# Widening in float32 on quarters of the array where no convolution runs beside it, and in four float16 products elsewhere

## The chip, the cores and the metric

The kernel runs on one core of a Trainium2 chip. The metric is the device time of one execution in microseconds (us); smaller is better. The core has five instruction streams that run on their own and wait for one another by semaphores: TensorE (PE, whose weight loads are listed as PEld), VectorE (DVE), ScalarE (ACT), GpSimd (POOL) and SyncE (SP, which only starts DMAs here).

## The reference

The input is 32 images of 64 channels and 112 x 112 pixels in float32. Two residual layers follow one another:

```
x = x + conv3x3(groupnorm(x), sign(weight) * alpha)
h = w_in (256 x 64) . groupnorm(x)                    # per pixel
h = irfft2(rfft2(8 x 8 patches of h) * fft_filt)      # per channel
h = depthwise 3x3 (h, w_dw)
x = x + w_out (64 x 128) . (gelu(h[:128]) * h[128:])  # per pixel
```

Group normalisation has 32 groups, so pairs of channels. The step that this document is about is `w_in`: 64 channels are widened to 256.

## The kernel before

Images are taken in 16 pairs (64 channels of either image make the 128 partitions) and each image in 14 strips of 8 rows. The kernel is a software pipeline over steps t = 0 to 13 for each pair: step t transposes and transforms strip t (`front`), widens, filters and evaluates strip t-1 (`mid`), interpolates strip t-2 (`up`) and projects strip t-3 (`done`). In steps 6 to 12 the binary convolution of the next pair runs as well, two strips in each; the last pair has no next one. So a strip whose widening falls in such a step is of kind "conv", each other of kind "plain": 105 strips are conv, and 119 are plain (7 of 14 in each of 15 pairs, and all 14 of the last pair). Statistics of the next pair (`bn_stats`) are taken by DVE in steps 0 to 4; the tiny matmuls that average the statistics over pairs of channels (`groups`) stand in steps 5 and 13.

Every engine's order is written out by hand in a function `image` for it, one branch for conv steps and one for plain ones. What one strip goes through in `mid`:

- `pixels` (ACT, line 464) copies the transposed strip to the tile xT; `forward_transform` (PE, line 930) turns it into the patch basis with float32 matmuls on four quarters of the array (64 rows and 64 columns each); `spectrum` (ACT, line 469) copies the result back to the same tile, then called xf.
- `spectrum_high` (ACT, line 478) rounds xf to float16, xf_hi; `spectrum_low` (POOL, line 351) makes the rest, xf_lo. w_in is held in the same way as win_hi and win_lo.
- `widened` (PE, line 941), in four groups of two, two, two and one of the strip's seven blocks of 16 columns, called W0, W1, W2 and W3 here. In a plain step their order is W3, W2, W1, W0. A block takes four products in float16 (hi.hi, lo.hi, hi.lo, lo.lo), each for both images on the upper and the lower half of the array's rows, which run side by side.
- `filtered` (DVE, line 690) multiplies each group with the filter into hf. W1 waits until the filtered W3 has left its PSUM banks, and W0 until the filtered W2 has.
- `evaluated` (PE, line 953), float32 on quarters of the array, in four groups for each image; `weighted` (DVE, line 697) multiplies each into one of three buffers of v32; `high_nodes` (ACT, line 487) and `low_nodes` (POOL, line 357) split it into v_hi and v_lo in float16.
- `interpolated` (PE, line 971) in the step after; then `carried0` and `gated` (DVE, 706, 713, 722), `gelu`, `keep0` and `keep1` (ACT, 507, 511, 516); `projected` (PE, 985), `lifted` (ACT, 494), `residual` (POOL, 364).

A group of v is written here as (image, group), so v(1,3) is the first of the second image. POOL's order in a plain step is residual, v_lo(0,3), residual, v_lo(0,2), (0,1), (0,0), (1,3), then xf_lo, then v_lo(1,0), (1,1), (1,2). The reuse of the three buffers of v32 ties DVE to POOL: `weighted` (1,3) waits until v_lo(0,2) is done, (1,0) until (0,1) is, and the next strip's (0,3) and (0,2) until v_lo(1,1) and (1,2) are:

```
V_BUF = {"plain": [{3: 0, 2: 1, 1: 2, 0: 0}, {3: 1, 0: 2, 1: 0, 2: 1}],
...
                nc.gpsimd.tensor_tensor(xf_lo[:], xf[:], xf_hi[:], ALU.subtract).then_inc(pool_xl, 1)
```

Of the kernel before, what the change touches and what calls it, by code (L numbers as in the profile page):

```python
# [8 lines left out]
ALU = mybir.AluOpType  # L9

P = 8
C = 64
C2 = 256
HC = 128
# [57 lines left out]
def shape_constants():  # L72

    basis, picks = patch_basis()
    pick = np.zeros((P * (P // 2 + 1), BPX))
    for patch in range(2):
        for f, (a, b) in enumerate(picks):
            pick[a, patch * P * P + f] += 0.5
            pick[b, patch * P * P + f] += 0.5
    samples_at, taps_at, back = toom_cook()  # L80
    nodes = np.zeros((P * P, 128))
    nodes[:, :POINTS] = basis.T @ np.kron(samples_at, samples_at).T

# [11 lines left out]
def build(nc, x, conv_w, alpha, w_in, w_dw, filt, w_out, forward, pick, pair, apart, identity, nodes, taps, ext, out):  # L95
    B, _, H, W = x.shape
    PAIRS = B // 2
    STRIPS = H // ROWS
# [8 lines left out]
    IMGS = 2  # L107
# [25 lines left out]
    with ctx:  # L133
        def sb(name, shape, dt=F32):
            return ctx.enter_context(nc.sbuf_tensor(name, shape, dt))
# [51 lines left out]
        filt_sb = v32[0:NF, 0, 1, 0, :]  # L187
        win_sb = v32[:, 2, 0, 0, :]
        c_taps = v32[0:9, 0, 0, 1, 0:128]
# [57 lines left out]
        pe_out = sem("pe_out")  # L247
        N_CONST = 15
        N_CONV = 4
# [33 lines left out]
        def _(sp):  # L283
# [10 lines left out]
            for dst, src in ((c_fwd[:], forward), (c_pick, pick), (c_pair[:], pair), (c_apart[:], apart), (c_id[:], identity),  # L294
                             (c_nodes[:], nodes), (c_taps, taps), (ext32, ext), (filt_sb, filt), (wdw_sb, w_dw),
                             (wout_sb[:], w_out), (win_sb[0:C], w_in), (win_sb[C:128], w_in)):
                sp.dma_start(dst, src).then_inc(dma_const, 16)
# [31 lines left out]
        def _(pool):  # L329
# [37 lines left out]
            def image(n, par, prev, front, more):  # L367
                for t in range(STRIPS if front else OUT):
                    mid = item(n, t, MID, prev, front)
                    done = item(n, t, OUT, prev, front)  # L370
                    if more and CONV_FROM <= t <= CONV_TO:
# [21 lines left out]
                    else:  # L393
# [10 lines left out]
                        if mid:  # L404
# [3 lines left out]
                            low_nodes(mid[0], mid[1], 1, 3)  # L408
                        if front:
                            spectrum_low(n, t)  # L410
# [20 lines left out]
        def _(act):  # L431
# [86 lines left out]
            def image(n, par, prev, front, more):  # L518
                for t in range(STRIPS if front else OUT):
# [3 lines left out]
                    if more and CONV_FROM <= t <= CONV_TO:  # L523
# [42 lines left out]
                    else:  # L566
# [20 lines left out]
                        if front:  # L587
                            spectrum(n, t, BANK_P)
                            spectrum_high(n, t)
                        if mid:  # L590
# [30 lines left out]
        def _(dve):  # L621
# [12 lines left out]
            def groups_x(n):  # L634
                dve.wait_ge(pe_grpx, n + 1)
                nc.vector.tensor_copy(groupx[:], Z[:, 0:3]).then_inc(dve_grpx, 1)
                dve.wait_ge(dve_grpx, n * 4 + 1)
                nc.vector.scalar_tensor_tensor(out=varx[:], in0=groupx[:, 2:3], scalar=groupx[:, 2:3],
                                               in1=groupx[:, 1:2], op0=ALU.mult, op1=ALU.add).then_inc(dve_grpx, 1)
                dve.wait_ge(dve_grpx, n * 4 + 2)  # L640
                nc.vector.tensor_scalar(vex[:], varx[:], 0.0, GN_EPS, ALU.max, ALU.add).then_inc(dve_grpx, 1)

            def shift_x(n):
                dve.wait_ge(pool_rstdx, n + 1)
                nc.vector.scalar_tensor_tensor(out=nbx[:], in0=groupx[:, 0:1], scalar=-1.0, in1=rstdx[:],
                                               op0=ALU.mult, op1=ALU.mult).then_inc(dve_grpx, 1)
# [5 lines left out]
            def groups_1(n):  # L652
                dve.wait_ge(pe_grp1, n + 1)
                nc.vector.tensor_copy(group1[:], Z[:, 0:3]).then_inc(dve_grp1, 1)
                dve.wait_ge(dve_grp1, n * 4 + 1)
                nc.vector.scalar_tensor_tensor(out=var1[:], in0=group1[:, 2:3], scalar=group1[:, 2:3],
                                               in1=group1[:, 1:2], op0=ALU.mult, op1=ALU.add).then_inc(dve_grp1, 1)
                dve.wait_ge(dve_grp1, n * 4 + 2)
                nc.vector.tensor_scalar(ve1[:], var1[:], 0.0, GN_EPS, ALU.max, ALU.add).then_inc(dve_grp1, 1)

            def shift_1(n):
                dve.wait_ge(pool_rstd1, n + 1)
                nc.vector.scalar_tensor_tensor(out=nb1[:], in0=group1[:, 0:1], scalar=-1.0, in1=rstd1[:],
                                               op0=ALU.mult, op1=ALU.mult).then_inc(dve_grp1, 1)
# [197 lines left out]
            nc.vector.tensor_copy(c_ext[:].rearrange("p a b -> p (a b)"), ext32).then_inc(dve_prep, 1)  # L862
            nc.vector.tensor_copy(win_hi[:], win_sb).then_inc(dve_prep, 1)
            dve.wait_ge(dve_prep, 3)
            nc.vector.tensor_tensor(win_lo[:], win_sb, win_hi[:], ALU.subtract).then_inc(dve_prep, 1)
            dve.wait_ge(pe_mult, 1)
# [18 lines left out]
        def _(pe):  # L885
            def groups(channels):
                nc.tensor.matmul(Z[:, 0:2], c_pair[:], channels[:], start=True, stop=True)
                return nc.tensor.matmul(Z[:, 2:3], c_apart[:], channels[:, 0:1], start=True, stop=True)

# [44 lines left out]
            def widened(b, s, grp, bank):  # L934

                k0, k1 = GROUPS[grp]
                pe.wait_ge(pool_xl, b * STRIPS + s + 1)
                for k in range(k0, k1):
                    for part, (xf, win) in enumerate(((xf_hi, win_hi), (xf_lo, win_hi), (xf_hi, win_lo), (xf_lo, win_lo))):
                        for r in range(IMGS):  # L940
                            last = nc.tensor.matmul(PS[:, bank + r, (k - k0) * C2:(k - k0 + 1) * C2],  # L941
                                                    xf[r * C:(r + 1) * C, k, :], win[r * C:(r + 1) * C, :],
                                                    start=part == 0, stop=part == 3)
                last.then_inc(pe_hf, 1)
# [310 lines left out]
```

## Time and profile before

| | |
|---|---|
| median of 3 runs | 5405.63 us (5405.21 to 5406.29) |
| the profiled execution, its own time | 5406.3 us |
| its span, first to last instruction | 5404.5 us |
| granted TensorE clock, mean | 0.996 of full speed (2.4 GHz) |
| instructions | 201429 |
| DMA, mean | 41 GB/s |

The profile is of one execution. Times of instructions are from the span's start. A matmul in float32 appears as two records, each with its weight load. A record's duration includes the way through the array, so consecutive ones overlap, and what a group of matmuls costs PE is the distance from its first start to the first start of what follows, not its busy time. "Idle before" names what ended an engine's wait, inferred from semaphores; the chain of waits follows the last instruction back through what released it.

### The profile page before, as it was taken

The page shows a single profiled execution, that of the slowest core. Times are in us where ns is not written, and L with a number is a line of the kernel's source. Part 1 is how long each engine was busy: PE and PEld are TensorE (multiplying, and loading weights), DVE is VectorE, ACT ScalarE, POOL GpSimd, SP SyncE. Part 2 cuts the span into 40 slices and gives each one's busy share as a digit, 9 for nine tenths or more (in the row PEclk, how much of TensorE's full clock was granted, in tenths as well). Part 3 has the DMA queues.
Part 4 walks back from the last instruction along what each step waited for, and adds up shares of the span by engine and source line. Part 5 has one row for each costly group of instructions (what it writes and reads, how often), then busy time and mean ns, then how long its engine had stood idle before and what let it go on. Part 6 is the DMA issues. An engine that isn't in the chain of part 4 may idle for free.

```text
span 5404.5 us, 201429 instructions
## 1 busy us (share of the span) xinstructions
PE 5202.6 (96%) x88868; PEld 3195.1 (59%) x88868; DVE 4642.3 (86%) x5703; ACT 3739.5 (69%) x4866; POOL 4643.1 (86%) x2727
## 2 busy tenths in 40 slices
PE   5999999999999999999999999999999999999998
PEld 4565655656556565565656556565665655656554
DVE  6889888888888888888898888988889888888876
ACT  3766767677676766767767676676766767677675
POOL 3889889898888988889888898888989889898898
PEclk9999999999999999999999999999999999999999
DMA  2011110110101111010010101101011110110000
GB/s 103 19 50 42 38 44 29 53 40 37 54 22 50 40 40 53 19 57 36 36 53 32 48 33 39 54 36 43 33 50 40 40 42 31 50 43 20 23 26 26
DMA packets 43953, 219.31 MB, mean 41 GB/s; under 512 B 5366, under 2 KB 6104, under 8 KB 36952
## 3 DMA queue, kind: packets, MB, share of 16 engines
q1 hardware_dynamic: 43096, 206.42, 9.9%
q8 instruction: 716, 11.73, 0.9%
q14 instruction: 141, 1.16, 0.1%
HBM read 103.64 MB, written 102.76 MB: 38 GB/s over the span
## 4 chain that ended last, share of the span: by engine, by line
PE 69%; DVE 15%; POOL 7%; issue 5%; ACT 3%; DMA 0%; DVEq 0%; SPq 0%; POOLq 0%; ACTq 0%
PE PS L953 20%; PE PS L971 17%; PE PS L912 14%; PE PS L941 10%; POOL v_lo L357 6%; DVE v L697 5%; PE PS L985 5%; DVE hf L690 4%; DVE g L722 2%; PE PS L921 2%; ACT v_hi L487 2%; DVE bn L628 2%; DVE PS L713 1%; ACT carry L516 1%; POOL xf_lo L351 0%
## 5 line engine op out<-in xcount | busy, mean ns | idle before, releaser
L357 POOL TENSOR_TENSOR v_lo<-v,v_hi 128x1024 f16<-128x1024 f32 (+1 forms) x1792 | 3354.6, 1898 | 455.4 <-ACT v_hi L487 455.0
L697 DVE TENSOR_TENSOR v<-PS,smul 128x1024 f32<-128x1024 f32 (+1 forms) x1792 | 1910.4, 1086 | 361.6 <-POOL v_lo L357 200.9
L487 ACT ACTIVATE v_hi<-v 128x1024 f16<-128x1024 f32 (+1 forms) x1792 | 1646.8, 944 | 717.5 <-DVE v L697 561.9
L953 PE MATMUL PS<-hf,c_nodes 64*64 64x512 f32 (+1 forms) x14336 | 1659.7, 556 | 70.4 <-DVE v L697 57.0
L971 PEld LDWEIGHTS PS<-c_ext,v_hi 128*128 128x128 f16 x14336 | 1129.9, 97 | 507.2 <-ACT carry L511 165.0
L971 PE MATMUL PS<-c_ext,v_hi 128*128 128x100 f16 (+2 forms) x14336 | 1258.9, 203 | 9.7 <-issue 4.1
L971 PE MATMUL PS<-c_ext,v_lo 128*128 128x100 f16 (+2 forms) x14336 | 1250.6, 202 | 0.0
L971 PEld LDWEIGHTS PS<-c_ext,v_lo 128*128 128x128 f16 x14336 | 1118.2, 97 | 1.2
L690 DVE TENSOR_TENSOR hf<-PS,mult 128x1024 f32<-128x1024 f32 (+1 forms) x896 | 954.8, 1086 | 86.7 <-PE PS L941 66.2
L953 PEld LDWEIGHTS PS<-hf,c_nodes 64*64 64x64 f32 x14336 | 406.8, 131 | 623.1 <-DVE v L697 219.7
L912 PE MATMUL PS<-S_hi,csign 64*64 64x448 f16 (+2 forms) x8640 | 746.8, 336 | 9.4 <-POOL S_lo L346 9.4
L912 PE MATMUL PS<-S_lo,csign 64*64 64x448 f16 (+2 forms) x8640 | 748.0, 337 | 0.0
L464 ACT ACTIVATE xT<-PS 128x896 f32<-128x896 f32 x224 | 205.6, 918 | 638.9 <-PE PS L921 638.9
L722 DVE TENSOR_TENSOR g<-PS,gel 128x912 f32<-128x912 f32 (+1 forms) x448 | 496.3, 1108 | 58.7 <-DVE PS L713 2.0
L346 POOL TENSOR_TENSOR S_lo<-n,S_hi 128x896 f16<-128x896 f32 x224 | 411.0, 1835 | 150.7 <-ACT S_hi L448 150.7
L351 POOL TENSOR_TENSOR xf_lo<-xT,xf_hi 128x896 f16<-128x896 f32 x224 | 425.5, 1900 | 83.4 <-ACT xf_hi L478 83.4
L941 PE MATMUL PS<-win_hi,xf_hi 64*128 64x256 f16 x3136 | 435.8, 274 | 59.0 <-DVE hf L690 33.1
L507 ACT ACTIVATE gel<-PS 128x912 f32<-128x912 f32 (+1 forms) x448 | 413.5, 923 | 110.1 <-DVE PS L706 109.0
L985 PE MATMUL PS<-g,wout_sb 128*64 128x448 f32 (+2 forms) x1792 | 445.6, 574 | 4.0 <-DVE g L722 2.3
L941 PE MATMUL PS<-win_hi,xf_lo 64*128 64x256 f16 x3136 | 429.1, 270 | 0.0
L941 PE MATMUL PS<-win_lo,xf_hi 64*128 64x256 f16 x3136 | 429.1, 270 | 0.0
L941 PE MATMUL PS<-win_lo,xf_lo 64*128 64x256 f16 x3136 | 429.0, 269 | 0.0
(74 smaller groups left out, 5846.0 us busy)
## 6 DMA issues: line engine op xcount, KB each, us to landing
out_x<-Xa SPq DMA_DIRECT2D x96, 448.0 KB, 2.5
out_x<-Xb SPq DMA_DIRECT2D x96, 448.0 KB, 2.5
Xa<-in_x SPq DMA_DIRECT2D x8, 2240.0 KB, 9.0
Xb<-in_x SPq DMA_DIRECT2D x8, 2240.0 KB, 8.9
Xa<-in_x SPq DMA_DIRECT2D x8, 1792.0 KB, 7.7
Xb<-in_x SPq DMA_DIRECT2D x8, 1792.0 KB, 6.8
Xa<-in_x SPq DMA_DIRECT2D x8, 1344.0 KB, 5.9
Xb<-in_x SPq DMA_DIRECT2D x8, 1344.0 KB, 6.7
```

Source lines behind the costliest of these rows:

```text
L351: nc.gpsimd.tensor_tensor(xf_lo[:], xf[:], xf_hi[:], ALU.subtract).then_inc(pool_xl, 1)
L357: nc.gpsimd.tensor_tensor(v_lo[:, img, :, k0:k1, :], v32[:, V_BUF[kind(b, s)][img][grp], :, 0:k1 - k0, :], v_hi[:, img, :, k0:k1, :], ALU. ...
L487: nc.scalar.activation(v_hi[:, img, :, k0:k1, :], v32[:, V_BUF[kind(b, s)][img][grp], :, 0:k1 - k0, :], ACT.Copy).then_inc(act_vhi[img], 1)
L507: nc.scalar.activation(gel[:, :, r0:r1, :], Y[:, :, r0:r1, :], ACT.Gelu).then_inc(act_y0, 1)
L690: nc.vector.tensor_tensor(hf[:, :, k0:k1, :], PS[:, bank:bank + 2, 0:(k1 - k0) * C2].rearrange("p i (k c) -> p i k c", c=C2), mult[:].unsq ...
L697: nc.vector.tensor_tensor(v32[:, V_BUF[kind(b, s)][img][grp], :, 0:k1 - k0, :], PS[:, bank:bank + 2, 0:(k1 - k0) * C2].rearrange("p i (k c ...
L722: nc.vector.tensor_tensor(g[:, img, r0:r1, :].rearrange("p r (b c) -> p b r c", c=YC), Y[:, :, r0:r1, :], gel[:, :, r0:r1, :], ALU.mult).t ...
L912: last = nc.tensor.matmul(PS[c * C:(c + 1) * C, bank + h, i0 * W:(i0 + m) * W], csign[r * C:(r + 1) * C, tap, :], S[r * C:(r + 1) * C, row ...
L941: last = nc.tensor.matmul(PS[:, bank + r, (k - k0) * C2:(k - k0 + 1) * C2], xf[r * C:(r + 1) * C, k, :], win[r * C:(r + 1) * C, :], start= ...
L953: last = nc.tensor.matmul(PS[points, bank + side, 0:(k1 - k0) * C2], c_nodes[half, points], hf[half, img, k0:k1, :].rearrange("p k c -> p ...
L971: last = nc.tensor.matmul(Y[:, b0, :, col - b0 * YC:end - b0 * YC], v[:, img, patch % 2, patch // 2, half * HC:(half + 1) * HC], c_ext[:, ...
L985: last = nc.tensor.matmul(Z[img * C:(img + 1) * C, 0:(r1 - r0) * HALF_W], wout_sb[:], g[:, img, r0:r1, 1 + q * HALF_W:1 + (q + 1) * HALF_W ...
```

## The change

Strips of kind "plain" are widened with float32 matmuls directly from xf and w_in, each image's 64 channels on one half of the rows and each half of a block's columns on one half of the array's columns: four matmuls for a block in place of eight. `spectrum_high` and `spectrum_low` are left out for these strips, so ACT and POOL lose one instruction in 119 steps each, and `pool_xl` counts conv strips alone (`xl_count`). The widening then waits for `act_xf`, and `pixels`, which overwrites xf, waits for the widening (`pe_hf`). w_in in float32 needs a tile of its own that lasts; the room comes from the constant `c_apart`, in whose place the identity and the pair matrix with its sign turned are applied one after the other: a third tiny matmul in `groups`. Conv strips are widened as before.

```
-    return {"forward": np.concatenate([basis, basis]), "pick": pick, "pair": pair, "apart": np.eye(HC) - pair, "identity": np.eye(HC),
+    return {"forward": np.concatenate([basis, basis]), "pick": pick, "pair": -pair, "identity": np.eye(HC),
...
-        c_apart = sb("c_apart", [128, 128])
+        win_sb = sb("win_sb", [128, C2])
...
+        def xl_count(b, s):
+            return (STRIPS // 2) * b + min(max(s - CONV_FROM + MID, 0), STRIPS // 2) if b < PAIRS - 1 else (STRIPS // 2) * b
...
             def spectrum_low(n, s):
-                pool.wait_ge(act_xh, n * STRIPS + s + 1)
+                pool.wait_ge(act_xh, xl_count(n, s + 1))
...
-                        if front:
+                        if front and kind(n, t) == "conv":
                             spectrum_low(n, t)
...
             def pixels(n, s, bank):
                 act.wait_ge(pe_xT, n * STRIPS + s + 1)
                 if n or s:
-                    act.wait_ge(pool_xl, n * STRIPS + s)
+                    act.wait_ge(pe_hf, 4 * (n * STRIPS + s))
+                    if xl_count(n, s):
+                        act.wait_ge(pool_xl, xl_count(n, s))
...
                             spectrum(n, t, BANK_P)
-                            spectrum_high(n, t)
+                            if kind(n, t) == "conv":
+                                spectrum_high(n, t)
...
-                return nc.tensor.matmul(Z[:, 2:3], c_apart[:], channels[:, 0:1], start=True, stop=True)
+                nc.tensor.matmul(Z[:, 2:3], c_id[:], channels[:, 0:1], start=True, stop=False)
+                return nc.tensor.matmul(Z[:, 2:3], c_pair[:], channels[:, 0:1], start=False, stop=True)
...
             def widened(b, s, grp, bank):
                 k0, k1 = GROUPS[grp]
-                pe.wait_ge(pool_xl, b * STRIPS + s + 1)
-                for k in range(k0, k1):
-                    for part, (xf, win) in enumerate(((xf_hi, win_hi), (xf_lo, win_hi), (xf_hi, win_lo), (xf_lo, win_lo))):
...
+                if kind(b, s) == "plain":
+                    pe.wait_ge(act_xf, b * STRIPS + s + 1)
+                    for k in range(k0, k1):
+                        for r, side in ((0, 0), (1, 1), (0, 1), (1, 0)):
+                            last = nc.tensor.matmul(PS[side * P * P:(side + 1) * P * P, bank + r, (k - k0) * C2:(k - k0 + 1) * C2],
+                                                    xf[r * C:(r + 1) * C, k, side * P * P:(side + 1) * P * P],
+                                                    win_sb[r * C:(r + 1) * C, :], start=True, stop=True)
+                else:
+                    pe.wait_ge(pool_xl, xl_count(b, s + 1))
...
```

PE's order where the change moves it, in a step 5, before (W1's second block, the statistics' matmuls, W0):

```order
L941 MATMUL PS<-win_hi,xf_hi 128x256 x2
L941 MATMUL PS<-win_hi,xf_lo 128x256 x2
L941 MATMUL PS<-win_lo,xf_hi 128x256 x2
L941 MATMUL PS<-win_lo,xf_lo 128x256 x2
L887 MATMUL PS<-mvx,c_pair 128x2
L888 MATMUL PS<-mvx,c_apart 128x1
L941 MATMUL PS<-win_hi,xf_hi 128x256 x2
```

And after, the same place (the first row is W3, W2 and W1 together, the last W0):

```order
3426 L949 MATMUL PS<-win_sb,xT 64x256 x20
3427 L894 MATMUL PS<-mvx,c_pair 128x2
3428 L895 MATMUL PS<-mvx,c_id 128x1
3429 L896 MATMUL PS<-mvx,c_pair 128x1
3430 L949 MATMUL PS<-win_sb,xT 64x256 x8
```

A block's eight matmuls of 64 rows by 128 columns have become four of 64 by 64, and one tiny matmul with a full load of 128 columns has come between W1 and W0.

POOL's order from a plain step 4 into step 5 (its residual pair, four groups of v_lo, xf_lo, three groups), before:

```order
146 L364 TENSOR_TENSOR Xb<-g,Xb 128x8x56
147 L357 TENSOR_TENSOR v_lo<-v,v_hi 128x2x256
148 L364 TENSOR_TENSOR Xb<-g,Xb 128x8x56
149 L357 TENSOR_TENSOR v_lo<-v,v_hi 128x2x512 x3
150 L357 TENSOR_TENSOR v_lo<-v,v_hi 128x2x256
151 L351 TENSOR_TENSOR xf_lo<-xT,xf_hi 128x896
152 L357 TENSOR_TENSOR v_lo<-v,v_hi 128x2x512 x3
153 L337 TENSOR_TENSOR rstdx<-vex,m_half 128x1
```

And after:

```order
135 L367 TENSOR_TENSOR Xb<-g,Xb 128x8x56
136 L360 TENSOR_TENSOR v_lo<-v,v_hi 128x2x256
137 L367 TENSOR_TENSOR Xb<-g,Xb 128x8x56
138 L360 TENSOR_TENSOR v_lo<-v,v_hi 128x2x512 x3
139 L360 TENSOR_TENSOR v_lo<-v,v_hi 128x2x256
140 L360 TENSOR_TENSOR v_lo<-v,v_hi 128x2x512 x3
141 L340 TENSOR_TENSOR rstdx<-vex,m_half 128x1
```

xf_lo is gone from between v_lo(1,3) and v_lo(1,0). In step 5 itself it stays, because strip 5 is widened in step 6, a conv step; in step 12 it goes.

## Rows read from the trace of the kernel before

**Rows 1.** The page, busy time of each engine over the span.
```profile
PE 5202.6 (96%) x88868; PEld 3195.1 (59%) x88868; DVE 4642.3 (86%) x5703; ACT 3739.5 (69%) x4866; POOL 4643.1 (86%) x2727
```
**Rows 2.** Windows: length; PE, PEld, DVE, ACT, POOL busy. Last-pair, statistics, conv step.
```profile
5163.06:5183.64 20.58, 19.66 (x324) 11.71 (x322) 16.20 (x19) 14.86 (x21) 18.81 (x11) 1.00 0.06 25
2145.11:2165.64 20.53, 19.51 (x321) 11.85 (x319) 18.82 (x25) 14.47 (x21) 18.61 (x13) 1.00 0.06 22
2258.90:2285.44 26.54, 26.43 (x479) 16.19 (x477) 22.77 (x29) 18.72 (x24) 22.45 (x13) 1.00 0.05 19
```
**Rows 3.** The chain of waits through a last-pair step: start, us, what.
```profile
5168.46 1.88 PE PS L953 x16
...
5172.65 0.56 PE PS L941 x8
...
5175.42 1.05 PE PS L941 x16
```
**Rows 4.** Timeline of POOL, the same step: start, us, operation, idle before.
```profile
5163.07 7.46 POOL L357 TENSOR_TENSOR v_lo<-v,v_hi 128x1024 f16<-128x1024 f32 x4 [1.43 <-ACT v_hi L487]
5170.49 1.90 POOL L351 TENSOR_TENSOR xf_lo<-xT,xf_hi 128x896 f16<-128x896 f32 x1
5172.36 6.32 POOL L357 TENSOR_TENSOR v_lo<-v,v_hi 128x1024 f16<-128x1024 f32 x3
```
**Rows 5.** Timeline of DVE, v(0,2) of the next strip in that step.
```profile
5179.45 1.22 DVE L697 TENSOR_TENSOR v<-PS,smul 128x1024 f32<-128x1024 f32 x1 [0.17 <-PE PS L953]
```
**Rows 6.** The chain of waits, a step with statistics.
```profile
2145.17 1.86 POOL xf_lo L351
2147.03 6.29 POOL v_lo L357 x3
2153.32 0.65 DVE v L697
```
**Rows 7.** Timeline of PE: W3's first pair, W2's first, W0's first, what follows W0.
```profile
5172.59 0.28 PE L941 MATMUL PS<-win_hi,xf_hi 64*128 64x256 f16 x2
5173.03 0.27 PE L941 MATMUL PS<-win_hi,xf_hi 64*128 64x256 f16 x2
...
5175.42 0.28 PE L941 MATMUL PS<-win_hi,xf_hi 64*128 64x256 f16 x2 [0.39 <-DVE hf L690]
...
5176.40 0.22 PE L971 MATMUL PS<-c_ext,v_hi 128*128 128x100 f16 x1
```
**Rows 8.** Timeline of PE: evaluated groups of 256 and 512 columns, and what follows.
```profile
2388.04 0.66 PE L953 MATMUL PS<-hf,c_nodes 64*64 64x256 f32 x8
2388.53 0.99 PE L930 MATMUL PS<-c_fwd,xT 64*64 64x64 f32 x56
...
5165.99 1.09 PE L953 MATMUL PS<-hf,c_nodes 64*64 64x512 f32 x8 [0.53 <-DVE v L697]
5167.01 0.22 PE L971 MATMUL PS<-c_ext,v_hi 128*128 128x100 f16 x1
```
**Rows 9.** Timeline of DVE: after that 256-column group, and after W3.
```profile
2388.84 0.69 DVE L697 TENSOR_TENSOR v<-PS,smul 128x512 f32<-128x512 f32 x1 [0.29 <-PE PS L953]
5173.24 0.69 DVE L690 TENSOR_TENSOR hf<-PS,mult 128x512 f32<-128x512 f32 x1 [0.84 <-PE PS L941]
```
**Rows 10.** Timeline of PE: the statistics' second matmul of a step 5, then W0.
```profile
2191.07 0.36 PE L888 MATMUL PS<-mvx,c_apart 128*128 128x1 f32 x2
2191.36 0.28 PE L941 MATMUL PS<-win_hi,xf_hi 64*128 64x256 f16 x2
```
**Rows 11.** Groups by line: the float32 weight loads of the forward transform.
```profile
L930 PEld LDWEIGHTS PS<-c_fwd,xT 64*64 64x64 f32 x12544 | 225.2, 135 | 32.3 <-DVE v L697 4.1 <-ACT xT L464 1.5 <-issue 1.1
```
**Rows 12.** Timeline of PE, a step with statistics: its wait for v(1,3).
```profile
2161.16 1.09 PE L953 MATMUL PS<-hf,c_nodes 64*64 64x512 f32 x8 [0.64 <-DVE v L697]
```
**Rows 13.** Timeline of ACT: the next strip's pixels.
```profile
5181.18 0.92 ACT L464 ACTIVATE xT<-PS 128x896 f32<-128x896 f32 x1 [0.35 <-PE PS L921]
```
**Rows 14.** Timeline of DVE: filtered W3 in a step with statistics.
```profile
2147.83 0.69 DVE L690 TENSOR_TENSOR hf<-PS,mult 128x512 f32<-128x512 f32 x1 [0.16 <-PE PS L941]
```

More of the change, by code:

```diff
@@ L90, in shape_constants, with build @@
     pair = np.kron(np.eye(HC // 2), np.full((2, 2), 0.5))
-    return {"forward": np.concatenate([basis, basis]), "pick": pick, "pair": pair, "apart": np.eye(HC) - pair, "identity": np.eye(HC),
+    return {"forward": np.concatenate([basis, basis]), "pick": pick, "pair": -pair, "identity": np.eye(HC),
             "nodes": np.concatenate([nodes, nodes]), "taps": taps, "ext": ext}
-def build(nc, x, conv_w, alpha, w_in, w_dw, filt, w_out, forward, pick, pair, apart, identity, nodes, taps, ext, out):
+def build(nc, x, conv_w, alpha, w_in, w_dw, filt, w_out, forward, pick, pair, identity, nodes, taps, ext, out):
     B, _, H, W = x.shape
@@ L187, in build @@
         filt_sb = v32[0:NF, 0, 1, 0, :]
-        win_sb = v32[:, 2, 0, 0, :]
         c_taps = v32[0:9, 0, 0, 1, 0:128]
@@ L247, in build @@
         pe_out = sem("pe_out")
-        N_CONST = 15
+        N_CONST = 14
         N_CONV = 4
@@ L293, in _ @@
                 sp.dma_start(alpha_sb[r * C:(r + 1) * C], alpha).then_inc(dma_conv, 16)
-            for dst, src in ((c_fwd[:], forward), (c_pick, pick), (c_pair[:], pair), (c_apart[:], apart), (c_id[:], identity),
+            for dst, src in ((c_fwd[:], forward), (c_pick, pick), (c_pair[:], pair), (c_id[:], identity),
                              (c_nodes[:], nodes), (c_taps, taps), (ext32, ext), (filt_sb, filt), (wdw_sb, w_dw),
-                             (wout_sb[:], w_out), (win_sb[0:C], w_in), (win_sb[C:128], w_in)):
+                             (wout_sb[:], w_out), (win_sb[0:C, :], w_in), (win_sb[C:128, :], w_in)):
                 sp.dma_start(dst, src).then_inc(dma_const, 16)
@@ L408, in image @@
                             low_nodes(mid[0], mid[1], 1, 3)
-                        if front:
+                        if front and kind(n, t) == "conv":
                             spectrum_low(n, t)
@@ L588, in image @@
                             spectrum(n, t, BANK_P)
-                            spectrum_high(n, t)
+                            if kind(n, t) == "conv":
+                                spectrum_high(n, t)
                         if mid:
@@ L638, in groups_x @@
                 nc.vector.scalar_tensor_tensor(out=varx[:], in0=groupx[:, 2:3], scalar=groupx[:, 2:3],
-                                               in1=groupx[:, 1:2], op0=ALU.mult, op1=ALU.add).then_inc(dve_grpx, 1)
+                                               in1=groupx[:, 1:2], op0=ALU.mult, op1=ALU.subtract).then_inc(dve_grpx, 1)
                 dve.wait_ge(dve_grpx, n * 4 + 2)
@@ L644, in shift_x @@
                 dve.wait_ge(pool_rstdx, n + 1)
-                nc.vector.scalar_tensor_tensor(out=nbx[:], in0=groupx[:, 0:1], scalar=-1.0, in1=rstdx[:],
+                nc.vector.scalar_tensor_tensor(out=nbx[:], in0=groupx[:, 0:1], scalar=1.0, in1=rstdx[:],
                                                op0=ALU.mult, op1=ALU.mult).then_inc(dve_grpx, 1)
@@ L656, in groups_1 @@
                 nc.vector.scalar_tensor_tensor(out=var1[:], in0=group1[:, 2:3], scalar=group1[:, 2:3],
-                                               in1=group1[:, 1:2], op0=ALU.mult, op1=ALU.add).then_inc(dve_grp1, 1)
+                                               in1=group1[:, 1:2], op0=ALU.mult, op1=ALU.subtract).then_inc(dve_grp1, 1)
                 dve.wait_ge(dve_grp1, n * 4 + 2)
@@ L662, in shift_1 @@
                 dve.wait_ge(pool_rstd1, n + 1)
-                nc.vector.scalar_tensor_tensor(out=nb1[:], in0=group1[:, 0:1], scalar=-1.0, in1=rstd1[:],
+                nc.vector.scalar_tensor_tensor(out=nb1[:], in0=group1[:, 0:1], scalar=1.0, in1=rstd1[:],
                                                op0=ALU.mult, op1=ALU.mult).then_inc(dve_grp1, 1)
@@ L862, in _ @@
             nc.vector.tensor_copy(c_ext[:].rearrange("p a b -> p (a b)"), ext32).then_inc(dve_prep, 1)
-            nc.vector.tensor_copy(win_hi[:], win_sb).then_inc(dve_prep, 1)
+            nc.vector.tensor_copy(win_hi[:], win_sb[:]).then_inc(dve_prep, 1)
             dve.wait_ge(dve_prep, 3)
-            nc.vector.tensor_tensor(win_lo[:], win_sb, win_hi[:], ALU.subtract).then_inc(dve_prep, 1)
+            nc.vector.tensor_tensor(win_lo[:], win_sb[:], win_hi[:], ALU.subtract).then_inc(dve_prep, 1)
             dve.wait_ge(pe_mult, 1)
@@ L936, in widened @@
                 k0, k1 = GROUPS[grp]
-                pe.wait_ge(pool_xl, b * STRIPS + s + 1)
-                for k in range(k0, k1):
-                    for part, (xf, win) in enumerate(((xf_hi, win_hi), (xf_lo, win_hi), (xf_hi, win_lo), (xf_lo, win_lo))):
[L940 to L943, printed above, removed]
+                if kind(b, s) == "plain":
[7 more added lines that the diff above has]
+                    pe.wait_ge(pool_xl, xl_count(b, s + 1))
+                    for k in range(k0, k1):
+                        for part, (x16, win) in enumerate(((xf_hi, win_hi), (xf_lo, win_hi), (xf_hi, win_lo), (xf_lo, win_lo))):
+                            for r in range(IMGS):
+                                last = nc.tensor.matmul(PS[:, bank + r, (k - k0) * C2:(k - k0 + 1) * C2],
+                                                        x16[r * C:(r + 1) * C, k, :], win[r * C:(r + 1) * C, :],
+                                                        start=part == 0, stop=part == 3)
                 last.then_inc(pe_hf, 1)
```

## The prediction

> **What bounds the kernel now.** I read the page first: PE is busy for 96% of the span, DVE and POOL for 86% each [rows 1]. A share of that kind doesn't say who sets a step's length, so I read windows next. A conv step takes 26.54 us with PE busy in 26.43: PE alone sets it, and the change leaves its work as it is. The two plain steps take 20.58 and 20.53 us with PE idle in about one [rows 2]. There DVE's work differs by 2.6 us between a step of the last pair and one with statistics, and the length doesn't follow, so it isn't DVE's sum of work either. POOL has 18.8 us of work in the first and is idle for 1.8.
>
> So a plain step is a loop of waits, and the chain shows it [rows 3]: W3 on PE, filtered W3 and W2 on DVE, W0 on PE, interpolation and evaluation on PE, then v(0,2) and the gate on DVE, a carry and v_hi(0,2) on ACT, v_lo(0,2) on POOL (at 5163.07 [rows 4], and again 20.57 us later), v(1,3) on DVE, evaluated (1,0) on PE (5165.99 [rows 8]), and on through PE to the next W3. What the change touches must lie on this loop to count. W3 and W0 do. W2 and W1 don't: between 5173.24 and 5175.38 the loop runs through DVE, and W0 sits idle for 0.39 us for it [rows 7]. xf_hi and xf_lo aren't on the loop at all.
>
> **POOL and ACT: removed, and worth nothing here.** POOL loses 119 times 1.90 us, 226 us in all. In a plain step its xf_lo runs from 5170.49, after v_lo(1,3) [rows 4]. Behind it stand only v_lo(1,0), (1,1) and (1,2), which end at 5178.68. Who needs them? v(0,3) and v(0,2) of the next strip, for buffers. v(0,2) starts at 5179.45, and what it waited for is PE [rows 5]: a margin of 0.77 us. The groups that DVE really waits for, v_lo(0,2) and (0,1), stand ahead of xf_lo, and POOL had been idle for 1.43 us before them, waiting for ACT [rows 4]. Finishing 1.90 us sooner only makes that idle time longer. ACT's xf_hi lies in the same shadow. I take 0 for both; what is late next is unchanged. In step 12, a conv step, PE covers it.
>
> **Widening: four float32 quarters for eight float16 halves.** Before, a block costs 0.44 us of PE (5172.59 to 5173.03) [rows 7], so a strip's seven cost 3.08. No float32 quarter of 256 columns with changing weights on 64 columns has its row here, but two near ones stand: evaluated groups are the same shape, four quarters and 256 columns of float32, at 0.49 us start to start (2388.04 to 2388.53), and 1.02 for 512 columns when an interpolation follows [rows 8]. Half of 1.02 is 0.51, with what the change to the interpolation costs in it; two groups of 512 columns in a row take 1.88 us in the chain [rows 3], 0.47 for each 256 columns. So a block costs between 0.43 (the eight halves' price, if nothing is lost) and 0.66 (the whole busy time of a lone group, no overlap between blocks). I take 0.47, that of the evaluated groups, the same shape; both ends are kept for the range. PE's work for a strip then grows from 3.08 to about 3.3 us, but only what is on the loop counts:
> - W3: the first filter starts 0.65 us after W3's start now (5172.59 to 5173.24) [rows 7, 9]. A float32 group of 256 columns is followed by DVE after 0.80 (2388.04 to 2388.84) [rows 9]. That is +0.15.
> - W0: 0.98 us to the next start (5175.42 to 5176.40) [rows 7], against 1.02 for the 512 columns [rows 8]: +0.04.
> - W1 and W2 end 0.2 us later in all, inside DVE's two filters; W0 still waits for DVE. 0, and +0.05 for W1 where no wait is left ahead of W0.
>
> **The third tiny matmul.** From the second one's records to W0 it takes 0.29 us [rows 10], a change of the array's division in it. A third costs a little less, 0.27, between W1 and W0 in steps 5 and 13, where W0 starts right behind it: on the path.
>
> **The new waits.** The widening waits for xf, from which ACT made xf_hi before, so it comes sooner than what was waited for. `pixels` must wait for W0, which is followed at 5176.40, and it runs at 5181.18, behind transposes that PE does later anyway [rows 7, 13]. No cost. The constants lose one DMA before the start: 0.
>
> **Sum.** The 119 plain widenings fall into three sorts:
> - 15 without statistics or groups (14 of the last pair and its step 0): 0.15 + 0.04 = 0.19, makes 2.9 us.
> - 30 with the tiny matmuls (steps 5 and 13): 0.15 + 0.05 + 0.27 + 0.04 = 0.51, makes 15.3 us.
> - 74 with statistics (steps 0 to 4): DVE mostly comes to W3 later than PE has it ready. Of five such steps in a row one filter waited for W3, for 0.16 us [rows 14], and the others started without a wait: +0.15 for the one. In two the chain led on along PE after W0, +0.04 each. 0.23 in five, 0.05 each, makes 3.4 us.
>
> Together +21.6 us on the profiled execution's span of 5404.5, so 5426.1; with the 1.8 us around it 5427.9. That execution stood 0.7 us above the median of the runs, which makes 5427, and since every wait elsewhere can only swallow some of it, I say 5426 us, 0.4% slower. From no change a measurement of this kernel tells about 0.2%, or 11 us.
>
> **Where a page speaks against the change.** The forward transform loads seven times eight float32 weights of 64 columns for a strip, 135 ns each on average [rows 11], 7.6 us of loads, in 0.99 us [rows 8]: loads for one quarter run beside the matmuls and loads of others, and the sum takes them as hidden. The Trainium skill's page "TensorE: Matmul & The Clock Gate", Part 3, "The mechanism", says that a weight load overlaps a running matmul only when its row group differs. Here two quarters share each row half, so by that rule the blocks would not overlap. The trace disagrees for 64 moving columns; no row has it for 256 with weights that change from block to block.
>
> **The rivals.**
> - *Blocks don't overlap* (much slower). If each block has to drain before its successor's weights are in, it costs 0.66 us [rows 8]. W3 and W2 then take 2.0 us and W1 1.3, W0 starts 0.47 us later than now (3.30 after W3's start, not 2.83 [rows 7]), and takes 0.35 longer: 0.82 in 119 steps, +98 us, 5503 us. For it: two quarters with one row half. Against it: the forward transform's 0.14 us for a block. It decides from a block of 0.6 us on, where five of them outlast the 2.98 us in which DVE gets to W0.
> - *All of it is swallowed* (no change). DVE's own late arrival covers W3 and W0 in the 74 steps, the tiny matmul hides behind the filter of W2: the 15 others and a part of the 30 are left, +3 to +9 us, 5409 to 5415. For it: the idle microsecond that every plain step has [rows 2].
> - *POOL was the limit* (faster). The chain in a step with statistics runs through 8.2 us of POOL without a gap, xf_lo ahead of v_lo(1,0) to (1,2), straight to v(0,3) at 2153.32 [rows 6]. If that was a real wait, taking 1.9 us from it lets DVE go ahead, and what PE then loses is its wait for v(1,3), 0.64 us in such a step [rows 12]: 74 times 0.64 is 47 us, against the 18 us that the other two sorts cost, so 5377 us. It decides if v(0,3) starts with the end of v_lo(1,2). By the code it needs only v_lo(1,1), which had ended about 2.1 us before, and DVE had come from other work just then, so I take the two ends for a coincidence; and in the last pair, where DVE has time, nothing of the kind is seen [rows 5].
>
> **How the numbers follow.** My forecast, slower by 11 to 40 us: 0.55. All swallowed: 0.28. POOL the limit: 0.12. No overlap: 0.05. The range goes from 5406, the swallowed case with nothing left, to 5446: with a block at 0.55 us and not 0.47, W3 gives 0.08 and W0 0.16 more, and over 119 steps, part of it swallowed, that is up to 20 us. It leaves out the rival that is faster and the one that is much slower. Slower by over 0.2%: the forecast and the last, 0.60. Within: 0.28. Faster: 0.12.
>
> **What would show it.** In the profile after, a block should start 0.47 us after the one before it, the first filter 0.80 after W3's start, and a step of the last pair should take 20.77 us. Conv steps stay at 26.5. POOL's idle time should grow by 1.9 us in a plain step, ahead of v_lo(0,2), with ACT as the releaser. I am wrong if a plain step is shorter than 20.5 us, if W0 no longer waits for DVE in the last pair, or if DVE's waits for v_lo shrink by more than noise.

## The result, and the profile after

The changed kernel takes 5424.49 us (median of 6 runs, 5421.10 to 5427.24), beside 5405.42 us for the kernel before in 6 runs (5401.08 to 5406.29). The ratio is 1.0036, with a 95% interval of 1.0026 to 1.0046: slower by 19 us, and the interval doesn't hold 1. The profiled execution has a span of 5424.0 us, 19.5 us more than before.

The page of the changed kernel, busy time by engine, against [rows 1]:

```profile
PE 5231.7 (96%) x88932; PEld 3126.1 (58%) x88932; DVE 4632.1 (85%) x5703; ACT 3626.6 (67%) x4747; POOL 4425.2 (82%) x2608
```

POOL has lost 218 us of work and ACT 113, and the kernel is slower all the same. The windows of the changed kernel, a step of the last pair, one with statistics and a conv step, against [rows 2]. The columns are the same: length, then PE, PEld, DVE, ACT and POOL busy, the clock, the DMA share and rate.

```profile
5201.81:5222.54 20.73, 19.85 (x324) 11.07 (x322) 16.21 (x19) 13.91 (x20) 16.96 (x10) 1.00 0.07 25
2159.52:2180.38 20.86, 19.89 (x323) 11.07 (x327) 19.21 (x25) 13.81 (x19) 16.95 (x11) 1.00 0.05 21
2258.44:2284.99 26.55, 26.44 (x480) 16.12 (x477) 22.77 (x29) 18.72 (x24) 22.43 (x14) 1.00 0.05 20
```

The step of the last pair is 0.15 us longer, the conv step the same to 0.01. The second row is cut at another place of the pair than its counterpart in [rows 2], so their lengths aren't set against each other; the table below does that. The chain of waits in the changed kernel's last-pair step, against [rows 3]:

```profile
5186.49 1.88 PE PS L969 x16
...
5190.68 0.64 PE PS L949 x8
...
5192.35 1.13 DVE hf L697
...
5193.52 1.09 PE PS L949 x16
...
5200.79 0.95 ACT v_hi L492
...
5201.81 2.16 POOL v_lo L360
```

It is the same loop with the same stations; W3 and W0 stand on it as float32 records of line 949. PE's timeline of that step, and DVE's first and fourth filters below it, against [rows 7, 9]:

```profile
5190.61 2.57 PE L949 MATMUL PS<-win_sb,xT 64*64 64x256 f32 x40
5193.52 1.09 PE L949 MATMUL PS<-win_sb,xT 64*64 64x256 f32 x16 [0.34 <-DVE hf L697]
5194.55 0.22 PE L987 MATMUL PS<-c_ext,v_hi 128*128 128x100 f16 x1
```
```profile
5191.34 0.69 DVE L697 TENSOR_TENSOR hf<-PS,mult 128x512 f32<-128x512 f32 x1 [0.92 <-PE PS L949]
5191.95 0.39 DVE L713 TENSOR_TENSOR PS<-PS,carry 128x228 f32<-128x228 f32 x1
5192.25 3.65 DVE L697 TENSOR_TENSOR hf<-PS,mult 128x1024 f32<-128x1024 f32 x3
```

The first filter starts 0.73 us after W3 (5190.61 to 5191.34), where it was 0.65. W0 is followed after 1.03 us (5193.52 to 5194.55), where it was 0.98. Between the first filter and W0 lie 2.18 us, as before: that part is DVE's. W0 still waits for DVE, 0.34 us. Together 0.13 us more for each round, and the rest of the loop is unchanged. One more thing is in the last row: three filters in a row take 3.65 us, where the same three took 3.59 before (from 5174.15). The fourth now waits some 0.06 us longer for W0.

POOL's timeline of a last-pair step, against [rows 4]:

```profile
5201.81 13.76 POOL L360 TENSOR_TENSOR v_lo<-v,v_hi 128x1024 f16<-128x1024 f32 x7 [1.44 <-ACT v_hi L492]
5215.53 1.06 POOL L367 TENSOR_TENSOR Xb<-g,Xb 128x448 f32<-128x448 f32 x1
5218.92 1.16 POOL L360 TENSOR_TENSOR v_lo<-v,v_hi 128x512 f16<-128x512 f32 x1 [2.33 <-ACT v_hi L492]
```

All seven groups now run in a piece without xf_lo, and then POOL is idle: 2.33 us ahead of v_lo(0,3), where it was 0.33. Ahead of v_lo(0,2), the group that DVE waits for, it is idle for 1.44 us with ACT as the releaser, as before. The 1.9 us that were saved went into waiting. DVE's waits for v_lo, in total, times and longest, did not shrink; before, and after:

```profile
DVE v L697 <- POOL v_lo L357: 200.9, 328, 1.4
DVE v L704 <- POOL v_lo L360: 203.0, 327, 1.4
```

The statistics' matmuls of a step 5, against [rows 10]:

```profile
2195.11 0.36 PE L895 MATMUL PS<-mvx,c_id 128*128 128x1 f32 x2
2195.33 0.36 PE L896 MATMUL PS<-mvx,c_pair 128*128 128x1 f32 x2
2195.62 1.09 PE L949 MATMUL PS<-win_sb,xT 64*64 64x256 f32 x16
```

The third costs 0.22 us (2195.11 to 2195.33), right ahead of W0.

**A ruler finer than the run.** Whole runs of one kernel scatter by some 10 us (the kernel before by 5400.3 to 5410.0 in the 26 runs beside the first experiments), too much for terms of 3 to 6 us. The steps don't. I took the starts of ACT's copy `pixels`, once in each step, and of the distances between them the median over 14 pairs, all in us. A column says which widening lies in the distance. "Sum of a pair" is all 14 distances; "last pair" is one step of it.

| kernel | five with statistics (W of steps 0 to 4) | W of step 5 | W of step 13 | seven conv | sum of a pair | last pair |
|---|---|---|---|---|---|---|
| before | 102.74 | 20.66 | 18.10 | 189.78 | 331.28 | 20.59 |
| changed | 103.15 | 21.07 | 18.49 | 189.76 | 332.47 | 20.72 |
| third_alone | 102.74 | 20.89 | 18.32 | 189.77 | 331.72 | 20.57 |
| no_third | 103.17 | 20.85 | 18.26 | 189.75 | 332.03 | 20.72 |
| relief_alone | 102.69 | 20.88 | 18.32 | 189.77 | 331.66 | 20.57 |
| quarters_alone | 103.18 | 21.07 | 18.49 | 189.76 | 332.50 | 20.72 |
| early_vhi_before | 103.49 | 20.67 | 18.59 | 189.21 | 331.96 | 20.59 |
| early_vhi_after | 103.98 | 21.08 | 18.97 | 189.20 | 333.23 | 20.74 |
| mid_vhi_before | 101.69 | 20.37 | 18.10 | 189.40 | 329.56 | 20.29 |
| mid_vhi_after | 102.18 | 20.78 | 18.49 | 189.43 | 330.88 | 20.43 |
| all_quarters | 103.17 | 21.07 | 18.49 | 190.84 | 333.57 | 20.72 |

By it the change costs 1.19 us a pair, 17.9 in fifteen, and 0.13 in 14 steps of the last, 1.8: 19.7 us, beside 19.5 in the spans.

### The profile page after: what moved, and what is told of

Read it like the earlier page. It is cut to its first block, busy times and chain, and to the rows that moved or that the text cites. A ratio compares the mean times of both kernels' runs of the same rounds, so it can differ in the third digit from the quotient of the medians.

```text
span 5424.0 us, 201200 instructions
## 1 busy us (share of the span) xinstructions
PE 5231.7 (96%) x88932; PEld 3126.1 (58%) x88932; DVE 4632.1 (85%) x5703; ACT 3626.6 (67%) x4747; POOL 4425.2 (82%) x2608
## 4 chain that ended last, share of the span: by engine, by line
PE 73%; DVE 15%; issue 5%; POOL 4%; ACT 3%; DMA 0%; DVEq 0%; SPq 0%; POOLq 0%; ACTq 0%
PE PS L969 21%; PE PS L987 18%; PE PS L920 14%; PE PS L957 7%; DVE v L704 5%; PE PS L1001 5%; PE PS L949 5%; POOL v_lo L360 4%; DVE hf L697 3%; DVE g L729 2%; PE PS L929 2%; ACT v_hi L492 2%; DVE bn L635 2%; DVE PS L720 1%; ACT carry L521 1%
## 5 line engine op out<-in xcount | busy, mean ns | idle before, releaser
L704 DVE TENSOR_TENSOR v<-PS,smul 128x1024 f32<-128x1024 f32 (+1 forms) x1792 | 1910.7, 1086 | 375.0 <-POOL v_lo L360 203.0
L949 PE MATMUL PS<-win_sb,xT 64*64 64x256 f32 x6664 | 439.8, 389 | 30.9 <-DVE hf L697 28.9
L920 PEld LDWEIGHTS PS<-S_hi,csign 64*64 64x64 f16 x8640 | 319.1, 107 | 149.8 <-DVE v L704 33.2
L920 PEld LDWEIGHTS PS<-S_lo,csign 64*64 64x64 f16 x8640 | 321.7, 106 | 131.5 <-issue 27.6
L949 PEld LDWEIGHTS PS<-win_sb,xT 64*64 64x64 f32 x6664 | 219.5, 133 | 193.5 <-DVE hf L697 117.9
L499 ACT ACTIVATE g<-PS 128x448 f32<-128x448 f32 (+1 forms) x448 | 244.9, 547 | 68.1 <-PE PS L1001 66.0
```

Of the source, the lines that this page charges most:

```text
L704: nc.vector.tensor_tensor(v32[:, V_BUF[kind(b, s)][img][grp], :, 0:k1 - k0, :], PS[:, bank:bank + 2, 0:(k1 - k0) * C2].rearrange("p i (k c ...
L920: last = nc.tensor.matmul(PS[c * C:(c + 1) * C, bank + h, i0 * W:(i0 + m) * W], csign[r * C:(r + 1) * C, tap, :], S[r * C:(r + 1) * C, row ...
L949: last = nc.tensor.matmul(PS[side * P * P:(side + 1) * P * P, bank + r, (k - k0) * C2:(k - k0 + 1) * C2], xf[r * C:(r + 1) * C, k, side * ...
```

## The experiments

### One part at a time

**third_alone** is the kernel before with the third tiny matmul. It keeps the changed kernel's constants, signs and new wait of `pixels`, and widens and splits as before; the edit that counts:

```
                 nc.tensor.matmul(Z[:, 0:2], c_pair[:], channels[:], start=True, stop=True)
-                return nc.tensor.matmul(Z[:, 2:3], c_apart[:], channels[:, 0:1], start=True, stop=True)
+                nc.tensor.matmul(Z[:, 2:3], c_id[:], channels[:, 0:1], start=True, stop=False)
+                return nc.tensor.matmul(Z[:, 2:3], c_pair[:], channels[:, 0:1], start=False, stop=True)
```

> The kernel before with the third tiny matmul alone (identity, then the negated pair matrix), all widening and splitting as before. My theory: it stands on the loop of waits in steps 5 and 13, where 0.21 us were seen between the second and the third in the trace after. Step 5 and step 13 grow by 0.2 us each, all others stay, +6 us: about 5412 us. Rival (it hides behind the filter of W2): no step changes, 5405 us.

Measured: 5414.72 us, ratio 1.0017 (1.0008 to 1.0026). Step 5 grew by 0.23 us and step 13 by 0.22, and nothing else moved: 0.45 us in 15 pairs is 6.8 us. The median of the runs says 9 us, which is within their scatter of it. The rival, that it hides behind the filter of W2, falls. PE's timeline of a step 5 of this kernel, with float16 W0 behind it:

```profile
2194.12 0.36 PE L893 MATMUL PS<-mvx,c_id 128*128 128x1 f32 x2
2194.35 0.36 PE L894 MATMUL PS<-mvx,c_pair 128*128 128x1 f32 x2
2194.64 0.28 PE L947 MATMUL PS<-win_hi,xf_hi 64*128 64x256 f16 x2
```

Again 0.23 us, and W0 right behind it with no wait.

**no_third** takes it out of the changed kernel:

```
-                nc.tensor.matmul(Z[:, 2:3], c_id[:], channels[:, 0:1], start=True, stop=False)
-                return nc.tensor.matmul(Z[:, 2:3], c_pair[:], channels[:, 0:1], start=False, stop=True)
+                return nc.tensor.matmul(Z[:, 2:3], c_id[:], channels[:, 0:1], start=True, stop=True)
```

> The changed kernel without the third tiny matmul: only the identity is applied to the mean, so the group variance lacks its correction. My theory: steps 5 and 13 lose 0.2 us each, the five between and the last pair's stay as they are in the changed kernel: 5424 - 6 = 5418 us. Rival: the step lengths don't move, 5424 us.

Measured: 5417.87 us, ratio to the kernel before 1.0025 (1.0015 to 1.0035). Steps 5 and 13 lost 0.22 and 0.23 us, the others kept their lengths to 0.02. Put in and taken out, the matmul has the same price: 6.7 of the 19.7 us.

**relief_alone** leaves the splits out where the change does, with the changed kernel's waits and third matmul, and widens in float16 throughout:

```
-                        if front:
+                        if front and kind(n, t) == "conv":
                             spectrum_low(n, t)
...
-                            spectrum_high(n, t)
+                            if kind(n, t) == "conv":
+                                spectrum_high(n, t)
...
+            nc.gpsimd.memset(xf_hi[:], 0.0).then_inc(pool_zero, 1)
+            nc.gpsimd.memset(xf_lo[:], 0.0).then_inc(pool_zero, 1)
```

> ACT's and POOL's splits left out for the 119 plain strips, the widening in four float16 products as before, which then reads stale xf_hi and xf_lo in plain strips; no third matmul is taken out (it is in). My theory: the relief is worth nothing, since xf_lo stands behind every v_lo that DVE waits for; only the third matmul's 0.2 us in steps 5 and 13 is seen, 5412 us, and POOL is idle 1.9 us more in each plain step. Rival (POOL was a limit, and the quarters cost more than I think): plain steps shorten by 0.1 us or more, 5400 us or less.

Measured: 5408.60 us, ratio 1.0005 (0.9996 to 1.0014). Its neighbour with the same third matmul is third_alone. Between the two one distance out of fourteen differs by more than 0.02 us, the one with W of step 3 (20.10 instead of 20.16): 0.06 us in 15 pairs is 1 us. The runs' medians differ by 6 us, which the steps don't bear out: by them third_alone should be 6.8 us above the kernel before and relief_alone 5.7, and the medians are 9.4 and 3.3 above it, either within the runs' scatter. In the last pair the step of the table has kept its length, and there too only the distance with W of step 3 is shorter (20.09 for 20.17). The window of a step of its last pair:

```profile
5208.07:5228.64 20.57, 19.66 (x323) 11.71 (x323) 16.20 (x19) 13.91 (x20) 16.95 (x11) 1.00 0.06 24
```

Against the first of [rows 2]: POOL 16.95 us for 18.81, ACT 13.91 for 14.86, and the step is 20.57 for 20.58. The rival that POOL was the limit falls. With it falls the reading of [rows 6] as a real wait: in the same step of relief_alone v_lo(1,2) ends at 2150.7 and v(0,3) starts at 2152.50, 1.8 us later, straight behind DVE's own statistics. The 0.06 us of W of step 3 can't come from that wait either, since the last pair, where v(0,3) waits for PE, has them as well; what they come from wasn't followed.

**quarters_alone** is the changed kernel with every strip split again, for nothing:

```
-                        if front and kind(n, t) == "conv":
+                        if front:
                             spectrum_low(n, t)
...
-                            if kind(n, t) == "conv":
-                                spectrum_high(n, t)
+                            spectrum_high(n, t)
```

> The changed kernel with ACT's and POOL's splits made for all strips again, though plain ones don't use them. My theory: the same as the changed kernel, 5424 us, step lengths equal to within 0.03 us. Rival (the relief gives something back): slower than that, by as much as the relief is worth.

Measured: 5424.32 us, ratio 1.0032 (1.0019 to 1.0044), and every column of the table within 0.03 us of the changed kernel. So with the quarters too the 226 us of POOL's work are worth nothing that these steps can tell. What the change costs is the quarters, 13 us (19.7 less 6.7), and the tiny matmul.

### What a block costs PE

**all_quarters** widens conv strips in the same way:

```
-                if kind(b, s) == "plain":
+                if True:
                     pe.wait_ge(act_xf, b * STRIPS + s + 1)
...
-                        if front and kind(n, t) == "conv":
-                            spectrum_low(n, t)
...
-                            if kind(n, t) == "conv":
-                                spectrum_high(n, t)
```

> The changed kernel with float32 quarters for the conv strips too, so no strip is split into xf_hi and xf_lo. Conv steps are bound by PE alone, so they show what the quarters cost PE with nothing to swallow it. My theory: a strip costs PE 0.2 to 0.25 us more, a conv step goes from 26.56 to about 26.8 us, plain steps stay: 5424 + 105 x 0.23 = 5448 us. Rival 1 (blocks do not overlap, 0.66 us each): 28.1 us. Rival 2 (the relief of POOL, busy for 22.5 of 26.5 us, counts where POOL has most to do): 26.56 or less.

Measured: 5439.60 us, ratio 1.0065 (1.0048 to 1.0081). A conv step went from 26.56 to 26.72 us. The window of one, and the chain of waits through its widening:

```profile
2267.10:2293.82 26.72, 26.62 (x480) 15.57 (x477) 22.77 (x29) 17.62 (x23) 20.60 (x13) 1.00 0.05 20
```
```profile
2301.90 1.06 PE PS L939 x16
2302.97 1.38 PE PS L977 x32
2304.34 2.50 PE PS L939 x40
2306.84 0.92 PE PS L991 x4
```

PE is busy in all but 0.1 us, so the 0.16 us are what a strip costs PE and nothing else. Spread over seven blocks that is 0.02 us each, so a block takes 0.46 us on average where the float16 products take 0.44. It isn't spread evenly. The third row of the chain, five blocks, takes 2.50 us; in the changed kernel, whose conv steps widen in float16, the same five take 2.38:

```profile
2323.27 2.38 PE PS L957 x40
```

From the starts of the matmuls, the first of these blocks takes 0.48 us in float32 and 0.45 in float16, but the second takes 0.43 and 0.44: a float32 block that follows its like costs no more, and the loss comes in where a group begins or ends. My 0.2 to 0.25 us for a strip were a little high, and with them the 5448 us, and rival 1 with its 0.66 us for a block is out by far. POOL lost 1.8 us of its 22.4 in these steps and the step grew, so rival 2 is out too.

### Is it the loop that I described?

The loop has one station where an engine is late only because of its order: v_hi(0,2) on ACT stands behind `pixels` and the carry `keep1`, and POOL is idle until it comes. If the loop is right, moving it must shorten plain steps, in either kernel, and the relief must still not count.

**early_vhi_before**, and the same edit in the changed kernel as **early_vhi_after**:

```
+                        if mid:
+                            high_nodes(mid[0], mid[1], 0, 2)
                         if front:
                             pixels(n, t, BANK_P)
                         if up:
                             keep1(up[0], up[1], 0)
                         if mid:
-                            high_nodes(mid[0], mid[1], 0, 2)
                             high_nodes(mid[0], mid[1], 0, 1)
```

> The kernel before with one ACT instruction moved: in plain steps v_hi(0,2) goes ahead of pixels and keep1 of the first image. It tests the loop: v_lo(0,2) was late for ACT alone, 1.4 us of idle POOL before it, and PE's wait for v(1,3), 0.54 to 0.64 us, hung on that. My theory: that wait goes, a step of the last pair falls from 20.59 to about 20.05 us (PE is then left with the wait ahead of W0, 0.39), steps with statistics by 0.2 to 0.5 since DVE has 19 us of work there; in all about 40 to 50 us less, 5360 us. Rival (POOL's sum of work is the limit): POOL has 18.8 of 20.6 us, the step stays within 0.1 us.

> The changed kernel with the same instruction moved. My theory: plain steps are then bound by PE and by the path from W3 over the filters to W0, where the quarters cost 0.08 + 0.05 us and the third matmul 0.21, so it stays slower than the same order in the kernel before by about the same 19 us: 5380 us. Rival (with the wait on ACT gone POOL becomes the limit, and the relief of 1.9 us is worth something at last): it is level with the kernel before in that order, or faster.

Measured: 5420.06 us, ratio 1.0026 (1.0015 to 1.0037), and 5433.82 us, ratio 1.0054 (1.0039 to 1.0068). Both expectations missed: it was to win 45 us and it lost 14. Between the two kernels lie 13.8 us by the runs and 21 by the steps, where 19 were expected. The last pair's step stayed at 20.59 to the hundredth. PE's timeline of early_vhi_before shows the reason:

```profile
5200.09 1.09 PE L954 MATMUL PS<-hf,c_nodes 64*64 64x512 f32 x8 [0.47 <-ACT xT L464]
5204.03 1.09 PE L954 MATMUL PS<-hf,c_nodes 64*64 64x512 f32 x8
```

The second row is evaluated (1,0), which used to wait 0.53 us for v(1,3): that wait is gone. But `pixels` now stands behind v_hi with its 1.04 us. Counted from the start of the transposes that it copies it comes 0.49 us later (1.51 us for 1.02; part of v_hi fits into time in which ACT was idle), and evaluated (0,0), the first row, needs the banks that `pixels` empties. It waits for 0.47 us. I had looked at whom v_hi delays and not at whom the instruction behind it does.

The last pair also shows where the lost time is. In two of its steps, with W of steps 2 and 3, there was less to win, and they grew from 20.40 to 20.91 us and from 20.16 to 20.48, as they did in the other pairs. In the first of them PE had no wait for v(1,3) before, in the second it had the one of the first row here. In their place came a wait for `pixels`, the second and third row:

```profile
5124.89 1.09 PE L953 MATMUL PS<-hf,c_nodes 64*64 64x512 f32 x8 [0.27 <-DVE v L697]
5116.76 1.09 PE L954 MATMUL PS<-hf,c_nodes 64*64 64x512 f32 x8 [0.47 <-ACT xT L464]
5137.67 1.09 PE L954 MATMUL PS<-hf,c_nodes 64*64 64x512 f32 x8 [0.51 <-ACT xT L464]
```

**mid_vhi_before** and **mid_vhi_after** put it between the two:

```
                         if front:
                             pixels(n, t, BANK_P)
+                        if mid:
+                            high_nodes(mid[0], mid[1], 0, 2)
                         if up:
                             keep1(up[0], up[1], 0)
                         if mid:
-                            high_nodes(mid[0], mid[1], 0, 2)
                             high_nodes(mid[0], mid[1], 0, 1)
```

> The kernel before with v_hi(0,2) moved ahead of keep1 only, behind pixels. In the first try pixels came 0.75 us later and PE waited 0.47 us for it, so the wait had only moved. Here pixels keeps its place, v_lo(0,2) starts 0.4 us sooner, and keep1 ends 0.17 us after PE is ready for what needs it. My theory: the loop shortens by about 0.35 us, the last pair's step from 20.59 to 20.2 us, 5370 to 5385 us in all. Rival (POOL's sum of work is the limit): nothing.

> The changed kernel with the same move. My theory: stays above the kernel before in that order by 15 to 20 us, since the quarters and the third matmul are on PE's path in either order. Rival (the relief counts once the loop is shorter): level or faster than the kernel before in that order.

Measured: 5376.97 us, ratio 0.9950 (0.9935 to 0.9965), and 5394.06 us, ratio 0.9977 (0.9967 to 0.9987). Both came out as expected, the first within its 5370 to 5385 us and the second 17.1 us above it, where 15 to 20 had been forecast. The last pair's step fell to 20.29 us, 0.30 less, and a pair's sum by 1.72. The chain of waits in mid_vhi_before, last pair:

```profile
5158.03 0.92 ACT xT L464
5158.95 0.94 ACT v_hi L487
5159.90 0.26 ACT carry L516
5160.15 0.05 issue
5160.20 1.45 PE PS L972 x32
```

POOL has left the loop. It now goes from `pixels` over v_hi and the carry to the interpolation on PE, three ACT instructions in a row. In POOL's timeline the idle time ahead of v_lo(0,2) has shrunk from 1.43 to 0.91 us:

```profile
5180.25 2.14 POOL L357 TENSOR_TENSOR v_lo<-v,v_hi 128x1024 f16<-128x1024 f32 x1 [0.91 <-ACT v_hi L487]
```

And the change costs the same in this order as in the old one: 1.32 us a pair and 0.14 a step of the last one, which makes 21.8 us by the steps and 17.1 by the runs. So even in the faster loop the relief isn't worth anything that these runs can tell. mid_vhi_before is faster than both kernels of this case, by 27 us than the one before.

## Why the prediction was right

5426 us was forecast and 5424.5 measured; the range was 5406 to 5446. Point by point:

- **What bounds a plain step.** Right. The loop is in the changed kernel's chain with the same stations, and an instruction moved on it changes the step, by 0.30 us.
- **POOL and ACT worth 0.** Right, by relief_alone (1 us) and quarters_alone (no difference). A detail was wrong: I expected POOL's idle time to grow ahead of v_lo(0,2). It grew ahead of v_lo(0,3), the first wait that POOL comes to when it is early.
- **W3: +0.15.** Half of it, 0.08. I took the distance from an evaluated group to DVE, 0.80 us, for that of a widened one. The group itself has the right length, 0.66 us, but what comes after it doesn't carry over. The chain in the changed kernel has this after evaluated (0,3) and (0,2), then after W3:

```profile
5197.53 0.03 issue
5197.56 0.02 DVEq L703
5197.58 0.04 issue
```
```profile
5191.32 0.02 issue
5191.34 0.04 DVE hf L697
```

  `weighted` waits for PE and for POOL's v_lo. The wait for PE stands in DVE's queue as an instruction of its own (line 703), the one for POOL with the product itself. `filtered` has one wait and no such instruction. From the end of PE's work to DVE's start the rows have 0.09 us for the one and 0.02 for the other, and the difference is the 0.07 that I had too much. No run changed this alone.
- **W0: +0.04.** 0.05.
- **A block: 0.47 us.** 0.46 on average, by all_quarters. A strip costs PE 0.16 us more and not 0.21.
- **Third matmul: +0.27.** 0.22, by two experiments. The 0.29 us from which I took it have the change of the array's division in them, and I took off too little.
- **The three sorts.** The 15 steps of the last pair's kind: 0.19 forecast, 0.13 measured. The 30 with tiny matmuls: 0.51 and 0.40. The 74 with statistics: 0.05 and 0.08, so 3.4 and 6.1 us. The third was too small because I overlooked one wait: where DVE leads, its fourth filter waits for W0, and that wait appeared: before the fourth filter it went from 0.02 to 0.09 us, the median over 14 pairs, for the strips widened in steps 0 to 4 as well as in the last pair. I had reckoned only with what follows W0 on PE.
- **The sum.** 21.6 us forecast, 19.7 measured in the steps: two terms too large by 4 us together, one too small by 3. That the total is nearer than its terms were is luck.
- **The rivals.** No overlap between blocks: out, by all_quarters. That rests on conv steps in which PE has no wait: the float32 loads, two quarters to a row half, are hidden at 256 moving columns as they were at 64. The page of the Trainium skill that spoke against it, "TensorE: Matmul & The Clock Gate", Part 3, "The mechanism", isn't borne out by this case as far as it says that a load overlaps a running matmul only when its row group differs. The same section's first paragraph also lets a load go ahead when it targets the background weight buffer, and that would allow what is seen; no run here tells which buffer a load went to. All swallowed: out; the third matmul shows in full, and in the 74 steps a wait appeared where I had seen cover. POOL the limit: out, by relief_alone and quarters_alone.
- **The signs of being wrong.** None came. A last-pair step is 20.73 us long, W0 still waits for DVE there, and DVE's waits for v_lo are 203.0 us in all where they were 200.9.

What stays open is why early_vhi_before lengthens the distance with W of step 13 by 0.5 us, while the first of the conv distances gets 0.5 us shorter. I followed the order of ACT in the last pair only.

## What to carry to other kernels

An engine at 86% can be given 226 us less to do and nothing happens, if what is taken away stands behind the instructions that others wait for. Ask of an instruction not how long it is but who waits for what stands after it in its queue. Price an edit at the places where one engine hands over to the next: a group there costs its latency to the last record and not only its share of the array's time. And moving an instruction ahead holds back those it passes, here `pixels` by 0.5 us behind one of 1.04, so look at whom they feed first.

## What the runs showed of the hardware that was not expected

- A block of float32 on four quarters, 64 rows by 64 columns with 256 moving columns and its own weights, takes 0.46 us on average in these kernels, and 0.43 behind another in the same group, against 0.44 us for eight float16 products on halves. Four exact products of split halves and one float32 product cost PE nearly the same.
- A step takes 0.5 to 3.5 us more than its kind at a few places in every execution, whatever the kernel, more than half of them between steps 9 and 10 of one pair or another (27.8 us for 26.56). One of them was followed. In the changed kernel's chain of waits it is a gap within a run of evaluated groups on PE for which the profile shows no wait:

```profile
2316.78 1.07 PE PS L969 x3
2317.85 0.21 issue
2318.06 1.94 PE PS L969 x13
```

Two groups take 3.2 us here and 1.95 elsewhere. Each execution whose steps I listed has four to seven such places, and early_vhi_before twelve, 3 to 11 us in all. They may make up a good part of the scatter between runs; that wasn't shown, and no run here says what they are.
